# Attention and gated feed-forward block on one core: reordered opening lists, fewer weight pieces a batch, blank matmuls in the last batch

## What is computed

```
x = x + layernorm(attention(layernorm(x)))
    scores = q k^T / sqrt(8) + rel_bias[clip(i - j + 128, 0, 256)]
    out    = softmax(scores) v,  then @ W_out + b_out
x = x + layernorm(ffn(layernorm(x)))
    h = silu(w1 x * s1) * (w2 x * s2)
    h = gelu(h1 h * s);  h = gelu(h2 h * s);  w3 h * s      (weights are -1, 0, 1)
```

## Time and profile before

| | |
|---|---|
| median of 3 runs | 310.52 us (310.03 to 310.61) |
| the profiled execution's own time | 310.07 us |
| its span in the trace | 308.3 us |
| PE, DVE, ACT, POOL busy | 278.4, 218.0, 205.6, 102.4 us |
| mean granted clock of PE | 0.949 |

### The profile page before, as it was taken

How to read it: one execution, slowest core, us unless ns; L and a number is a source line. 1 busy time by engine, 2 the same in 40 slices (tenths; PEclk the granted TensorE clock), 3 DMA queues, 4 the chain that set the end, 5 groups by cost and what they waited for, 6 DMA issues and landing times.

```text
span 308.3 us, 5129 instructions
## 1 busy us (share of the span) xinstructions
PE 278.4 (90%) x1857; PEld 183.7 (60%) x1857; DVE 218.0 (71%) x443; ACT 205.6 (67%) x315; POOL 102.4 (33%) x107
## 2 busy tenths in 40 slices
PE   8999679989999999999995999876899999999991
PEld 8665444645555555555553555434687888888870
DVE  4673866788789989989788559872754763574486
ACT  1777546678786877785874465955646988697750
POOL 6533010100610603906996931011752110510111
PEclk9999958999999999999998579989999999999997
DMA  6997401534032153470321000000000000010012
GB/s 178 306 202 131 172 1 43 201 88 105 9 99 72 48 187 115 154 215 14 104 72 51 22 0 1 4 1 2 1 0 2 0 0 0 2 34 0 3 35 72
DMA packets 21356, 21.17 MB, mean 69 GB/s; under 512 B 3664, under 2 KB 18768, under 8 KB 21072
## 3 DMA queue, kind: packets, MB, share of 16 engines
q1 hardware_dynamic: 20432, 20.52, 23.1%
q10 hardware_dynamic: 896, 0.29, 0.4%
HBM read 14.90 MB, written 5.64 MB: 67 GB/s over the span
## 4 chain that ended last, share of the span: by engine, by line
PE 50%; DVE 22%; ACT 8%; POOL 8%; issue 5%; SPq 3%; DMA 2%; ACTq 1%; POOLq 0%; DVEq 0%
PE place L1421 9%; PE place L1422 9%; DVE mx L678 7%; PE place L1231 6%; PE pv L1281 6%; PE place L1257 3%; ACT ring L992 3%; PE place L1223 3%; DVE y_and_z L613 2%; DVE stats L602 2%; DVE place L685 2%; PE place L1182 2%; POOL w_hi L562 2%; POOL w_lo L554 2%; POOL xn L564 2%
## 5 line engine op out<-in xcount | busy, mean ns | idle before, releaser
L678 DVE TENSOR_REDUCE mx<-place 128x4 f32<-128x1024 f32 x64 | 78.1, 1221 | 19.0 <-PE place L1231 18.1
L511 POOL TENSOR_TENSOR rstd<-mv,mhalf 128x2 f32<-128x2 f32 (+1 forms) x26 | 20.9, 805 | 158.5 <-DVE mv L610 158.5
L992 ACT ACTIVATE ring<-place 128x1024 f32<-128x1024 f32 x64 | 65.5, 1025 | 10.0 <-PE place L1268 5.3
L999 ACT COPY place<-raw 128x1024 f32<-128x1024 f32 x37 | 37.8, 1020 | 18.8 <-DVE mx L678 18.8
L1231 PE MATMUL place<-room,identr 128*128 128x512 f32 x128 | 49.5, 469 | 0.0
L1421 PE MATMUL place<-room,w_hi 128*128 128x512 f32 (+1 forms) x116 | 44.6, 387 | 0.7 <-DVE room L807 0.7
L1422 PE MATMUL place<-room,w_hi 128*128 128x512 f32 (+1 forms) x116 | 44.0, 382 | 0.0
L1281 PE MATMUL pv<-ring,vx 128*9 128x256 f32 x512 | 37.0, 411 | 2.4 <-ACT ring L992 2.4
L1257 PE MATMUL place<-room 33*128 33x256 f32 x256 | 33.7, 345 | 3.3 <-DVE place L685 1.8
L807 DVE TENSOR_TENSOR room<-ring,room 128x512 fp32r<-128x512 f32 x32 | 21.4, 690 | 18.6 <-ACT room L1082 18.6
L1223 PE MATMUL place<-room 33*128 33x256 f32 x256 | 29.1, 305 | 4.6 <-ACT ring L992 2.1
(11 more groups left out here) (138 smaller groups left out, 441.7 us busy)
## 6 DMA issues: line engine op xcount, KB each, us to landing
raw<-ext SPq DMA_DIRECT2D x8, 384.0 KB, 5.7
room<-q_parts SPq DMA_DIRECT2D x48, 64.0 KB
room<-k_parts SPq DMA_DIRECT2D x48, 64.0 KB
w_lo<-h SPq DMA_DIRECT2D x2, 1024.0 KB, 5.1
q_parts<-w_hi SPq DMA_DIRECT2D x4, 256.0 KB, 3.1
k_parts<-w_hi SPq DMA_DIRECT2D x2, 512.0 KB, 3.5
xs<-x SPq DMA_DIRECT2D x3, 256.0 KB, 5.6
w_lo<-w SPq DMA_DIRECT2D x3, 256.0 KB, 2.7
```

Of the source, the lines that this page charges most:

```text
L511: nc.gpsimd.tensor_tensor(rstd[:, at:at + width], mv[:, at:at + width, 1], mhalf[:, 0:width], ALU.pow).then_inc(rstd_set, 1)
L678: nc.vector.tensor_reduce(mx[:, s // RPAIRS, :, :, s % RPAIRS].rearrange("p i k -> p k i"), max_tile(b * PAIRS + s)[:, :, :].rearrange("p ...
L992: nc.scalar.activation(probs[:, s % PRING, :, :, :].rearrange("p k j n -> p (k j n)"), score_tile(b * PAIRS + s)[:, :, :].rearrange("p k n ...
L999: nc.scalar.copy(score_tile(i)[:, :, :].rearrange("p k (j n) -> p k j n", j=2), pair_windows(raw[:, :, :], i % PAIRS)).then_inc(bias_set, 1)
```

## The change

- **DVE's opening list**: only the first weight load is waited for (three semaphores in place of one); the moments of unit 1 and the normalize of unit 0 come ahead of the spreading; the half `(0,)` of the query weights is spread by DVE and the half `(1,)` by ACT. The normalize of unit 2 moves behind the first maximum, moments and normalize of unit 3 behind the third and fourth, the low parts of unit 2 behind maxima 6 and 7.
- **ACT's opening list**: the first negated maxima are taken ahead of the rows of pair 6; the high parts of unit 2 stand before and behind the rows of pair 7. SP sends the negated maxima of batch 0, ACT did so before.
- **SP**: the tables 6 and 7 are loaded ahead of the first stores.
- **POOL**: the inverse deviation of unit 3 comes behind table 5; `SPLIT_AT` gives 3 pieces to batches 4 and 5 and one to batch 6, in place of 4, 3 and none.
- **PE**: chunk 4's product in slot 6 comes ahead of the maxima product; in the last batch the scores and bias of pair 7 come ahead of the weighted sum of group 2; blanks (`BLANKS`) stand ahead of each weighted sum of the last batch and ahead of the third gate.
- **ACT's last batch**: the table load for Silu comes ahead of the copy of the last weighted sum.

```diff
-        SPLIT_AT = ((), (0,), (1,), (2, 3), (4, 5, 6, 7), (8, 9, 10), (), ())
+        SPLIT_AT = ((), (0,), (1,), (2, 3), (4, 5, 6), (7, 8, 9), (10,), ())
+        BLANKS = (2, 2, 2, 6, 6)
...
-            load_table(sp, 5)
+            for s in range(5, PAIRS):
+                load_table(sp, s)
...
             store_parts(1)
-            load_table(sp, 6)
             sp.wait_ge(parts_out[1], PARTS_OUT)
             row_dmas(1, 0, PAIRS, second_rows_in)
-            load_table(sp, 7)
             load_x(4)
+            send_mrow(sp, 0, 0)
             store_parts(2)
...
             for b in range(B):
-                if b > 0:
-                    send_mrow(sp, b, 1)
+                send_mrow(sp, b, 1)
...
             for s in range(PAIRS):
                 table_high(s)
+                if s == 5:
+                    x_inv_std(3)
...
             x_moments(0)
-            dve.wait_ge(qk_w_in, 48)
+            dve.wait_ge(qk_w_in[0], 16)
             nc.vector.tensor_scalar(wq_sb[:, :], wq_sb[:, :], scale, None, ALU.mult).then_inc(bq_scaled, 1)
-            nc.vector.tensor_scalar(bq_sb[:, 0:1], bq_sb[:, 0:1], scale, None, ALU.mult).then_inc(bq_scaled, 1)
+            x_moments(1)
+            x_normalize(0)
             dve.wait_ge(row_zeros, 1)
             dve.wait_ge(bq_scaled, 1)
-            spread_weights(nc.vector.tensor_copy, 0)
-            x_normalize(0)
+            spread_weights(nc.vector.tensor_copy, 0, (0,))
...
-            x_moments(1)
+            x_normalize(1)
...
+            act.wait_ge(row_zeros, 1)
+            act.wait_ge(bq_scaled, 1)
+            spread_weights(nc.scalar.copy, 0, (1,))
             keep_xT(0)
...
-            for s in range(2, PAIRS):
+            for s in range(2, PAIRS - 2):
                 take(s)
                 keep_rows(s)
-                if s == 5:
-                    keep_xT(2)
...
+            keep_xT(2)
+            take(PAIRS - 2)
+            minus_max(0, 0)
+            keep_rows(PAIRS - 2)
+            take(PAIRS - 1)
             q_and_k_high(2, 0)
-            minus_max(0, 0)
-            send_mrow(act, 0, 0)
+            keep_rows(PAIRS - 1)
             q_and_k_high(2, 1)
...
+            nc.scalar.activation(table_loaded[:, :], mhalf[:, 0:1], ACT.Silu)
             keep_weighted(B - 1, GROUPS - 1)
-
-            nc.scalar.activation(table_loaded[:, :], mhalf[:, 0:1], ACT.Silu)
...
             def weighted(b, g):
 
+                if b * GROUPS + g > 0:
+                    pe.wait_ge(oT_set, b * GROUPS + g)
+                if b + 1 == B:
+                    stream(pv, blank, blank, BLANKS[g])
                 pe.wait_ge(exp_done, b * PAIRS + (2 * g + 2))
...
-                    scores(b, s)
+                    if more or s not in BY_PE:
+                        scores(b, s)
+                    if s == 6 and 1 <= b <= 4:
+                        pe.wait_ge(mrow_set, b * RANGES + 3)
+                        if b == 1:
+                            x_T(4)
+                        if b == 2:
+                            pe.wait_ge(xT_set, 5)
+                        if b in (2, 3):
+                            q_and_k(4, b - 2)
+                        if b == 4:
+                            v(4)
                     if more:
                         max_scores(b + 1, s)
                         max_bias(b + 1, s)
-                    if s in BY_PE:
+                    if s in BY_PE and more:
                         score_bias(b, s)
+                    if s + 1 in BY_PE and not more:
+
+                        scores(b, s + 1)
+                        score_bias(b, s + 1)
...
-                whole(gate, 0, exact, (0, 1, 2))
+                whole(gate, 0, exact, (0, 1))
+                pe.wait_ge(oT_set, B * GROUPS)
+                stream(pv, blank, blank, BLANKS[GROUPS])
+                gate(0, 2, exact)
```

More of the change, by code:

```diff
@@ L212, in build @@
         ident_loaded = sem("ident_loaded")
-        qk_w_in = sem("qk_w_in")
+        qk_w_in = [sem(f"qk_w_in{i}") for i in range(3)]
         wv_in = sem("wv_in")
@@ L366, in wait_score_place, with spread_weights @@
                 eng.wait_ge(exp_done, i - 2)
-        def spread_weights(copy, i):
+        def spread_weights(copy, i, halves=range(2)):
             weights = (wq_sb, wk_sb)[i][:, :]
-            for half in range(2):
+            for half in halves:
                 src = bass.AP(tensor=weights.tensor, offset=weights.offset + half * PAIRS,
@@ L522, in _ @@
             x_inv_std(0)
-            pool.wait_ge(qk_w_in, 48)
+            pool.wait_ge(qk_w_in[1], 16)
             pool.wait_ge(row_zeros, 1)
@@ L534, in _ @@
                                         ALU.subtract).then_inc(table_lo_set, 1)
-            x_inv_std(3)
             x_inv_std(4)
@@ L665, in _ @@
                                     ALU.mult).then_inc(low_bias_set, 1)
-            x_moments(1)
+            x_normalize(1)
             dve.wait_ge(ident_loaded, 16)
             nc.vector.tensor_scalar(minus_ident[:, :], ident[:, :], -1.0, None, ALU.mult).then_inc(minus_set, 1)
+            dve.wait_ge(qk_w_in[2], 16)
+            nc.vector.tensor_scalar(bq_sb[:, 0:1], bq_sb[:, 0:1], scale, None, ALU.mult).then_inc(bq_scaled, 1)
             nc.vector.tensor_copy(identr[:, :], ident[:, :]).then_inc(identr_set, 1)
-            x_normalize(1)
             x_moments(2)
@@ L673, in _ @@
             q_and_k_low(1, 1)
-            x_normalize(2)
             def maxima(b, s):
@@ L741, in _ @@
                 if s == 0:
+                    x_normalize(2)
                     keep_v(0)
@@ L744, in _ @@
                     keep_v(1)
-                if s in (4, 5):
-                    q_and_k_low(2, s - 4)
+                if s == 2:
+                    x_moments(3)
+                if s == 3:
+                    x_normalize(3)
+                if s == 6:
+                    q_and_k_low(2, 0)
+            q_and_k_low(2, 1)
             keep_v(2)
-            x_moments(3)
-            x_normalize(3)
             def largest_low():
@@ L915, in _ @@
         def _(act):
-            for dst, src in ((wq_sb, wq), (wk_sb, wk), (bq_sb, bqk)):
-                act.dma_start(dst[:, :], src).then_inc(qk_w_in, 16)
+            for i, (dst, src) in enumerate(((wq_sb, wq), (wk_sb, wk), (bq_sb, bqk))):
+                act.dma_start(dst[:, :], src).then_inc(qk_w_in[i], 16)
             act.dma_start(brows_sb[:, :, :].rearrange("p a s -> p (a s)"), brows).then_inc(brows_in, 16)
@@ L1025, in _ @@
                         minus_max(b, 1)
-                        if b == 0:
-                            send_mrow(act, 0, 1)
                     if b == 0:
@@ L1179, in row_products @@
                 for i in range(2):
-                    if s == 0:
-                        pe.wait_ge(row_w_set[i], 2)
+                    pe.wait_ge(row_w_set[i], 2)
                     last = mm(bank[s % 2][:, i * S:(i + 1) * S], row_w[:, i, s, :], xT_of[0], start=(i == 0), stop=False,
@@ L1276, in weighted @@
                     pe.wait_ge(v_set, max(UNIT_OF[b] + 1, 3))
-                if b * GROUPS + g > 0:
-                    pe.wait_ge(oT_set, b * GROUPS + g)
                 for j in range(2):
@@ L1388, in _ @@
                             v(3)
-                    if s == 6 and 1 <= b <= 4:
-                        pe.wait_ge(mrow_set, b * RANGES + 3)
-                        if b == 1:
-                            x_T(4)
-                        if b == 2:
-                            pe.wait_ge(xT_set, 5)
-                        if b in (2, 3):
-                            q_and_k(4, b - 2)
-                        if b == 4:
-                            v(4)
                     if s == 5 and more:
```

## The result

The changed kernel takes 292.74 us (median of 4 runs, 292.38 to 293.34) against 310.45 (4 runs, 310.03 to 310.61): ratio 0.9433, 95% interval 0.9415 to 0.9452. The forecast was 292.3. One thing is needed for reading the numbers: on the chips of the experiments the kernel before shows two groups of times, near 305 and near 310 us; the four above are all of the upper group, and the ratios of the experiments are taken against the lower one (those of e9, e10 and e11 against nine runs of which three lie near 309). So the gain is 17.7 us where the kernel before takes 310, and by the same numbers some 12.5 us (a ratio near 0.96, an estimate) where it takes 305.

What follows compares the result with a forecast made beforehand. TensorE was taken as the bound, its waits followed by 1.2 GHz stretches. Terms -8.8 (containing -0.7), 0, -7.7, +1.0 and -2.7 gave -18.2 on 310.07: 291.9, plus 0.45 for the median, forecast 292.3 us; range 288.5 to 297.5.

Steps and rivals of the forecast that it cites:

- First rows, -0.7: Opening: second normalize can start 1.2 us earlier; between 0 and 1.2, a gain of 0.7 us was taken.
- To the fourth scores, -8.8: Batch 0, maxima to fourth scores: VectorE's reordered chain starts them at 40.2, not 48.93; minus 8.8 us, 0.7 contained.
- The 4.3 us as the price of a slow clock: Opening, 37.9 to 48.1 us: half of 8.62 us of slow work, expected back if the clock is not full.
- Chunk 4, 0: Batches 1 to 4: products ahead of the maxima cost 0, bound 0.3 us a batch either way, 1.2 in all.
- Pieces, -7.7 and +1.0: Fewer GpSimd weight pieces in batch 4 shorten batch 5 by 7.7 us; piece 10 lengthens batch 6 by 1.0.
- Last batch, -2.7: Last batch: last exponential 2.0 us earlier, and the third gate behind it 0.7 more; minus 2.7 us.
- Rival (b): One slow stretch remains or appears at another place: 294 to 299 us; chance 0.25.
- Rival (c): Opening: first rows of maxima or second rows land late, TensorE idles and may run slow: 298 us; chance 0.07.
- Rival (e): Batches 1 to 4: products ahead of the maxima start slow stretches, 7.7 us per stall, 323 us for four; chance 0.04.

Runs made afterwards that it cites:

- e9: Changed kernel with VectorE's moments and norm of the fourth unit behind the maximum of pair 5, not behind maxima 2 and 3; 299.29 us.
- e10: Changed kernel with the high and low parts of the third chunk of queries and keys in their old places; 296.02 us.
- e11: Changed kernel with chunk 4's products back behind the maxima, no last-batch blanks, and GpSimd's pieces held until VectorE's first norm of the batch; 291.60 us.
- e8: Changed kernel with VectorE's norm of unit 0 and the spread of the first weights ahead of unit 1's moments; 292.53 us.
- e2: Kernel before with the opening's reordered lists alone; 300.46 us, ratio 0.9769.
- e1: Kernel before with the new table of weight pieces and nothing else; 301.27 us, ratio 0.9898.
- b1: Kernel before, unchanged, profiled once more on a chip of the experiments; 305.61 us.
- e6: Changed kernel with GpSimd made to wait, ahead of each batch's pieces, for VectorE's first state of that batch; 292.25 us.
- e7: Changed kernel with the last batch's scores and bias of pair 7 put back behind the weighted sum of group 2; 293.94 us.
- e3: Changed kernel with chunk 4's product put back behind the maxima of pair 6, nothing else; 291.84 us.
- e4: Changed kernel with no blanks in the last batch; 292.41 us.

## Why the prediction was right, and where not

1. **First rows, -0.7.** Measured 0 by the product of pair 6. The step that failed took the tokens' landing at 5.5 us as fixed: with the new list the first norm stands behind tokens that may land later (6.3 here), and in the new list ScalarE and TensorE hang on the first norm and no longer on the second (e8).
2. **To the fourth scores, -8.8.** Measured -7.8. (The sum's 8.8 is 48.93 - 40.2 = 8.7, rounded up.) The chain was laid out rightly, and e10 and e2 bear it out; its start was 0.7 late by step 1, and TensorE's part of it took 3.4 and not 3.2. That the clock would stay full was right. Of the 7.8, 5.8 is VectorE's chain (third scores at 37.77 and not 43.53) and 2.0 the full clock behind it. The 4.3 us as the price of a slow clock took half of all the work in the stretch; it is 2.0 to 2.8, since TensorE waits for VectorE in the first part of it (e1). Two things the layout had missed: GpSimd's list as the thing that norm 3 holds up (e9), and that norm 3 would take 3.75 us beside GpSimd's casts, where the slack covered it by luck.
3. **Chunk 4, 0.** Measured +0.24 a batch, 0.96 in all, inside the bound of 0.3. I had looked for a late maximum; the loss is in the wait for ScalarE's row of negated maxima, which nothing covers now.
4. **Pieces, -7.7 and +1.0.** Measured -7.62 and, with the blanks' 0.59 taken off, +0.19; against the 16.12 of b1, which no long slow stretch precedes, the second is +0.53, of which e6 gets 0.39 back. The first is right in size and cause, with 5.4 of it slow clock and 2.2 wait. It depends on the run, as the last batch's term does: against b1 it is 3.8. The norm is 1.74 as forecast, but I took its whole length as loss. That batches 2 to 5 carry the same overlap already (1.66 to 1.74 us in the changed kernel) I had not used: 0.25 was to be had in batch 5.
5. **Last batch, -2.7.** Measured -3.05. Last exponential 2.4 earlier against its projection (forecast 2.0), gates 0.6 (forecast 0.7). 1.6 of it is the slow stretch that does not come; against b1, which has none either, it is 1.4. The blanks' 0.48, which I rounded away, fell mostly into batch 6.

Against the profiled execution the forecast was 1.4 us too low (291.9 for 293.34): +0.6 in the opening, +1.0 in batches 1 to 4, +0.1 in batch 5, -0.2 in batch 6, -0.35 in the last, +0.3 in the rest. On the medians 0.4 of it is left, because the profiled execution of the changed kernel lies 0.6 above its median and that of the kernel before 0.4 below. That the number came out within 0.4 us is thus partly luck; the mechanisms in steps 2, 4 and 5 are not. Rival (b), one slow stretch left, did not happen, and e7 shows how near it was: with the old order in the last batch it can come. Rival (c): TensorE shows no wait for the second rows or the maxima row; the last rows were issued at 22.7 and landed within 6.9, by 29.6 (forecast 29.9); they start 2.0 us later than before, where the forecast had 2.7. Rival (e) had the right place and the wrong price: the products ahead of the maxima do cost, in each of four batches, but 0.24 us and not 7.7, since they start no slow stretch.

## What to carry to other kernels

Where an engine's wait is followed by a stretch of lower granted clock, price both: here a 2.2 us delay cost 7.6 in one execution and 3.8 in another, and with idle work for TensorE in the wait the trace shows no slow stretch and 2.2 us. Half of a slow stretch is too much where the engine waits for another in it: the 10 us stretch of the opening cost 2 to 3. Ask of every instruction moved which engines' lists hang on its result, the third engine's too, and put a small operation that others wait for ahead of, not beside, long GpSimd work. Where distances are compared, mind what precedes them: batch 6 looked unchanged in e1 only because the slow stretch ahead of it had stretched it in before. For edits of some tenths of a us, compare distances between milestones inside the trace; they repeat to 0.05 us where medians of runs spread by 1.

## What the runs showed of the hardware

The same kernel with the same wait of 3.2 to 3.3 us had a slow stretch of 13.6 us behind it in one execution (and e2, with a wait of 3.30, one of 13.6) and of 3.4 in another. That is 3.9 us; with a slow stretch of the last batch that also comes or not, 1.6, it makes up the two groups of times 5 us apart. Without these stretches the spread is small: before lies in 304.1 to 311.3 on the chips of the experiments, and each of e3, e4, e6, e8 and e11, variants of the changed kernel on the same chips, within 1.9 us, all between 291.5 and 293.7. Blank work was of no use to the clock where it stayed full without it, with waits of up to 1.51 us (e4), and in e7 a slow stretch of 3.4 us came in spite of it. Two to four VectorE normalizes beside GpSimd's casts took about three times as long as alone: 1.74 us for 0.60, 3.75 for 1.12.
